# A four-layer graph network on one core: layer 0 adds its rows into a table of x, and layer 1 normalises what it gathers

## The reference

```python
h = relu(layernorm(x)); x = x + L0(h)   # two products and segment sums over dst, relu of each
h = relu(layernorm(x)); x = x + L1(h)   # sum of neighbours, relu(h @ W1.T + b1) @ W2.T + b2, layernorm
h = relu(layernorm(x)); x = x + L2(h)
h = relu(layernorm(x)); x = x + L3(h)

def gnn_layer(x, W, b, src, dst):       # L0 is this twice, with W1 and W2
    h = x @ W.T + b
    agg = segment_sum(h[src], dst)
    return relu(agg)
```

## Time and profile before

| | us |
|---|---|
| time, median of 3 | 2800.5 (2799.15 to 2801.04) |
| span of the profiled execution | 2943.3 |
| p, 0 to 62 | 62 |
| r, 62 to 323 | 261 |
| o, 323 to 384 | 61 |
| a, 384 to 712 | 328 |
| b, 712 to 1175 | 463 |
| c, 1175 to 1774 | 599 |
| d, 1774 to 2363 | 589 |
| f, 2363 to 2943 | 580 |

### The profile page before, as it was taken

The page is one execution under the profiler, slowest core; times in us unless marked ns, Lnnn a source line. Parts: engine busy times, 40 slices in busy tenths (PEclk is TensorE's granted clock), DMA queues, the critical chain, the costliest instruction groups (busy, mean ns, idle before and its releaser), DMA issues. The chain is left out here.

```text
span 2943.3 us, 48010 instructions
## 1 busy us (share of the span) xinstructions
PE 2538.7 (86%) x13886; PEld 2157.9 (73%) x13886; DVE 2010.9 (68%) x5233; ACT 1401.3 (48%) x2905; POOL 1737.8 (59%) x1867
## 2 busy tenths in 40 slices
PE   4555269997878776799999987999999979999998
PEld 3444158886767665799999986888888768888886
DVE  7777656663545444487878886888888846666666
ACT  1555235543656554555555533433333245555554
POOL 1666335554565555577777756877777555555554
PEclk9999999998999898899999998999999989999999
DMA  8777533334333443434334324433333245555553
GB/s 251 203 206 208 159 106 112 111 119 121 104 113 119 129 129 106 126 116 131 109 114 121 112 73 129 129 117 113 115 116 109 80 135 156 151 152 153 151 154 116
DMA packets 146046, 388.08 MB, mean 132 GB/s; under 512 B 34372, under 2 KB 34692, under 8 KB 145315
## 3 DMA queue, kind: packets, MB, share of 16 engines
q0 software_dynamic: 101408, 304.38, 35.0%
q1 hardware_dynamic: 43442, 80.04, 8.9%
q10 hardware_dynamic: 1056, 2.10, 0.2%
HBM read 261.83 MB, written 149.12 MB: 140 GB/s over the span
## 5 line engine op out<-in xcount | busy, mean ns | idle before, releaser
L824 PE MATMUL b_po<-parts,b_Thi 128*128 128x512 f32 x320 | 144.7, 452 | 72.0 <-issue 40.9
L1565 PE MATMUL c_pu<-c_Zhi,parts 128*128 128x256 f32 x640 | 182.9, 286 | 5.3 <-DVE c_Zlo L1490 5.3
L1567 PE MATMUL c_pu<-c_Zhi,parts 128*128 128x256 f32 x640 | 182.4, 285 | 0.0
L1566 PE MATMUL c_pu<-c_Zlo,parts 128*128 128x256 f32 x640 | 181.3, 283 | 0.0
L845 POOL DMA_INDIRECT f_Gsrc<-rows,indexS x80 | 79.2, 990 | 167.3 <-PE f_phsrc L2061 161.3
L1979 ACT ACTIVATE f_Mhi<-f_pm 128x512 fp32r<-128x512 f32 x80 | 47.9, 599 | 266.4 <-DVE f_pm L2012 259.8
L2003 DVE TENSOR_TENSOR f_Hlosrc<-f_phsrc,f_Hhisrc 128x512 fp32r<-128x512 f32 x80 | 55.4, 692 | 168.0 <-ACT f_Hhisrc L1973 137.3
L814 DVE SCALAR_TENSOR_TENSOR b_carry<-b_carry,keylastD,b_pt 128x4 f32<-128x4 f32 x80 | 17.4, 218 | 212.6 <-PE b_pt L1282 127.8
L1727 ACT CAST d_Hhi<-d_ph 128x512 fp32r<-128x512 f32 x80 | 46.8, 585 | 227.3 <-PE d_ph L1841 222.3
L849 POOL DMA_INDIRECT h<-a_rows,indexD x80 | 80.5, 1006 | 124.0 <-ACT a_rows L1148 116.5
L1457 ACT ACTIVATE c_pu<-c_pu,c_b1col 128x256 f32<-128x256 f32 x160 | 61.8, 450 | 164.6 <-PE c_pu L1567 164.6
(11 more groups left out here) (461 smaller groups left out, 9817.4 us busy)
## 6 DMA issues: line engine op xcount, KB each, us to landing
rows<-r_xt SPq DMA_DIRECT2D x40, 520.0 KB
h<-q_zerorow SPq DMA_DIRECT2D x80, 256.0 KB
r_xt<-in_x SPq DMA_DIRECT2D x80, 256.0 KB
selrowsD<-selD SPq DMA_DIRECT2D x1, 2640.0 KB
selrowsS<-selS SPq DMA_DIRECT2D x1, 2640.0 KB
q_keyrowD<-in_dst POOLq DMA_DIRECT2D x1, 2560.0 KB, 17.8
q_keyrowS<-in_src POOLq DMA_DIRECT2D x1, 2560.0 KB
o_wstage<-in_L_W ACTq DMA_DIRECT2D x2, 1024.0 KB
```

What stands on the lines that cost most here:

```text
L824: ins = pe.matmul(out, hi[:, c, :], whi[:, c, :], start=start and c == 0, stop=False, skip_group_check=preset)
L1565: pe.matmul(psum_u[:, o, :], g.Whi[2][:, c, cols], Zhi[:, c, :], start=c == 0, stop=False)
L1566: pe.matmul(psum_u[:, o, :], g.Whi[2][:, c, cols], Zlo[:, c, :], start=False, stop=False)
L1567: ins = pe.matmul(psum_u[:, o, :], g.Wlo[2][:, c, cols], Zhi[:, c, :], start=False, stop=c == C - 1)
```

## The change

- In r the pass over x is gone: its loads, statistics and stores. SP only writes zeros.
- Table `rows1` is replaced by `plain1`, with rows of 512, a row of zeros and 512 spare rows behind.
- In o the index column of the D order names for each row either its node or, where the row isn't the last of its key, a spare row: four small DVE steps more.
- In a, POOL gathers rows of x itself, eight tiles ahead. DVE takes statistics of each gathered tile, POOL makes scales and biases for four tiles at a time, and ACT normalises with them. SP copies x into `plain1` with 80 DRAM-to-DRAM transfers.
- In b, no row of x is gathered and nothing is normalised. POOL adds the relu'd rows to `plain1` with an accumulating indirect DMA (`add_rows`), tile by tile. The selection matrix is made by DVE in one operation (`select`) in place of two on ACT.
- In c, G and X come 512 wide from `plain1`. DVE takes the statistics of both, POOL makes four columns of scales and biases per pair (`scales_in`), and the second bias is put into PSUM by ACT ahead of the product (`preset`) and no longer added by DVE.
- d and f only change the names of their tables.

```diff
-                def statistics_x(T):
-                    dve.wait_ge(q_x[T.slot(RX)], 16 * (T.use(RX) + 1))
-                    ln.statistics(dve, T, xt[:, T.slot(RX), 0:D])
...
+def add_rows(pool, table, at_rows, rows):
+    return pool.indirect_dma_start(table, bass.IndirectOffsetOnAxis(ap=at_rows, axis=0), rows, None,
+                                   compute_op=ALU.add)
...
+                for t in range(NT):
+                    sp.wait_ge(s_rows, t + 1)
+                    sp.dma_start(g.x1[t * P:(t + 1) * P, :], io.x[t * P:(t + 1) * P, :]).then_inc(s_copy, 16)
...
-                if second:
-                    for u in range(RING):
-                        if u % QUAD == 0:
-                            at(i, u, -QUAD, RING, NT, scales)
-                        at(i, u, 4, RING, NT, start_fetch)
-                        at(i, u, 2, RING, NT, residual)
-                        at(i, u, -QUAD, RING, NT, store)
...
+                for u in range(U):
+                    at(i, u, -2, U, NT, store)
+                    if not second and (u + 3) % 4 == 0:
+                        at(i, u, 3, U, NT, scales)
+                    at(i, u, RG, U, NT, start_fetch)
...
-                dve.scalar_tensor_tensor(rows[:, r, 0:D], psum_o[s][:, :], 0.0, xr[x][:, :],
-                                         ALU.max, ALU.add).then_inc(s_rows, 1)
+                dve.tensor_scalar(rows[:, r, :], psum_o[s][:, :], 0.0, None, ALU.max).then_inc(s_rows, 1)
...
+            def scales_in(T):
+                J = item(T, 0)
+                some = slice(J.slot(8), J.slot(8) + 4)
+
+                wait(pool, s_Gn, T.t - 2)
+                wait(pool, s_own, T.t - 2)
+                ln_in.make_scales(pool, J, neg_half, scale_in[:, some])
+                ln_in.make_biases(pool, J, scale_in[:, some], bias_in[:, some])
...
                     at(i, pair, -2, U, NT, lengths_y)
+                    at(i, pair, 6, U, NT, scales_in)
                     for u in (pair, pair + 1):
                         at(i, u, 4, U, NT, keep_x)
...
+            def preset(T):
+
+                wait(act, s_rows, T.t - 3)
+                nc.scalar.copy(psum_o[T.slot(4)][:, :], b2[:, :]).then_inc(s_preset, 1)
...
-                dve.tensor_tensor(o, o, b2[:, :], ALU.add).then_inc(s_biased, 1)
...
+                    for u in (pair, pair + 1):
+                        at(i, u, 6, U, NT, norm_in)
+                        at(i, u, 6, U, NT, finish_in)
```

More of the change, by code:

```diff
@@ L331, in _ @@
                         sp.dma_start(g.sorted[k][row:row + 1, 0:1], sentinel[:, :]).then_inc(q_end, 16)
[L334 to L360, removed]
+                for rows in g.xs:
+                    sp.dma_start(rows[N + 1 - P:N + 1, :], zero_row[:, :]).then_inc(q_end, 16)
+                sp.dma_start(g.x1[N:N + 1, :], zero_row[0:1, 0:D]).then_inc(q_end, 16)
+                for n in range(ADD_RING):
+                    sp.dma_start(g.x1[N + 1 + n * P:N + 1 + (n + 1) * P, :], zero_row[:, 0:D]).then_inc(q_end, 16)
+                for t in range(NT // 2, NT):
+                    sp.wait_ge(q_pos["S"], 2 * (t - NT // 2) + 1)
+                    sp.dma_start(g.h1[t * P:(t + 1) * P, :], zero_row[:, 0:D]).then_inc(q_zero, 16)
                 sp.wait_ge(q_zero, 16 * NT)
-                sp.wait_ge(q_end, 16 * 7)
+                sp.wait_ge(q_end, 16 * (7 + ADD_RING))
             @block.vector
@@ L387, in pick @@
                             .then_inc(q_pos[k], 1)
-                def statistics_x(T):
-                    dve.wait_ge(q_x[T.slot(RX)], 16 * (T.use(RX) + 1))
-                    ln.statistics(dve, T, xt[:, T.slot(RX), 0:D])
[L393 to L398, removed]
-                def body(i):
[L401 to L409, removed]
-                straight(NT // RX, 1, 1, body)
+                def body(i):
+                    for u in range(U):
+                        at(i, u, 1, U, NT, before)
+                        at(i, u, 0, U, NT, pick)
+                straight(GR, 1, 1, body)
             @block.gpsimd
@@ L988, in layer0 @@
             s_preset = e.sem("s_preset")
-        neg_half = e.sb("neghalf", [P, QUAD], F32)
-        G = e.ring("G", U, [P, D if second else EXT], F32)
+        G = e.ring("G", RG, [P, D], F32)
+        if not second:
+            ln = Norm(e, "ln", True, 4)
+            neg_half = e.sb("neghalf", [P, 4], F32)
+            scale_in, bias_in = e.sb("scalein", [P, 8], F32), e.sb("biasin", [P, 8], F32)
         sel = e.ring("sel", 2, [P, P], F32)
@@ new lines, in scales @@
+            def scales(T):
+                some = slice(T.slot(8), T.slot(8) + 4)
+                wait(pool, s_Gn, T.t - 4)
+                ln.make_scales(pool, T, neg_half, scale_in[:, some])
+                ln.make_biases(pool, T, scale_in[:, some], bias_in[:, some])
+            def body(i):
+                for u in range(U):
+                    at(i, u, -2, U, NT, store)
+                    if not second and (u + 3) % 4 == 0:
+                        at(i, u, 3, U, NT, scales)
+                    at(i, u, RG, U, NT, start_fetch)
@@ L1081, in _ @@
-            pool.wait_ge(s_const, 4 if second else 3)
-            straight(NT // RING, 1, 1, body, between=W and (lambda i: W.low_part(pool, i)))
+            pool.wait_ge(s_const, 3)
+            straight(NT // RING, 2, 1, body, between=W and (lambda i: W.low_part(pool, i)))
             for s in range(RING):
@@ L1169, in _ @@
             else:
-                pipeline(act, GR, 1, 1, body, between=lambda i: W.high_part(act, i), first=2 * C + 2)
+                straight(GR, 2, 1, body, between=lambda i: W.high_part(act, i))
         @block.vector
@@ L1495, in norm_y, with norm_in, finish_in @@
             def norm_y(T):
-                o = psum_o[T.slot(4)][:, :]
                 dve.wait_ge(s_prod, T.t + 1)
-                dve.tensor_tensor(o, o, b2[:, :], ALU.add).then_inc(s_biased, 1)
-                dve.wait_ge(s_biased, T.t + 1)
-                ln_y.statistics(dve, T, o)
+                ln_y.statistics(dve, T, psum_o[T.slot(4)][:, :])
+            def norm_in(T):
+                s = T.slot(U)
+                for n, landed, tile in ((0, s_G, G), (1, s_X, X)):
+                    J = item(T, n)
+                    dve.wait_ge(landed[s], 16 * (T.use(U) + 1))
+                    wait(dve, ln_in.s_mean, J.t - 1)
+                    dve.sem_inc(tick, 1)
+                    ln_in.statistics(dve, J, tile[s][:, :])
+            def finish_in(T):
+                for n in range(2):
+                    ln_in.finish(dve, tick, item(T, n))
             def center(T):
```

230 lines of the change are left out of this document (82 added, 148 removed).

## The result

The changed kernel takes 2905.9 us (median of 4, 2904.03 to 2908.98) against 2800.26: the ratio is 1.0382, with a 95% interval of 1.0369 to 1.0395, slower by 105.6 us. The forecast was 2873, slower, with a range of 2750 to 2905. The side and the main mechanism hold; the size is 33 us short, and the time lies 0.9 us beyond the range.

The account below looks back on a forecast made before the run. PE was taken to pace a, c, d and f, something else r and b. Terms of -35 (r), +1 (o), +6 (a), -30 (b), +126 and +5 (c) gave +73 on 2800.5: 2873 us, range 2750 to 2905.

Parts of the forecast that it names:

- The ring in c: In c, POOL's power waits for DVE's variances of tiles POOL gathered last pass: 17.1 us a pair against 13.95, +126.
- the start: In c, statistics and power come ahead of the first sum: +5 us.
- The 142.8 us: Profiled span above the median before the change, assigned to that execution alone: 103 us in b, 40 in r.
- Rival 1: b's late starts also occur in timed executions and the change removes them: 2770 us, faster; chance 0.28.
- The gain is between 0 [...] and 56. I take 35: In r, removing the pass over x leaves POOL's transfers, 205 us against 261: taken as -35.
- the transfers' 205: In r, POOL's two indirect transfers a tile over 80 tiles take 205 us.
- +6: In a, first gather, statistics, POOL's power and ACT delay the start: +6 us, between 3 and 25.
- the 80 copies of SP add [...] to a DMA share of 0.35; hidden: In a, SP's copies add 2 × 256 KB a tile to the DMA load at no cost in time.
- It just fits: In a, DVE's added 1.0 us a tile fits its 1.04 us of waiting for PE, within the 3.86 us tile.
- -30: b, without the 103 us, goes from 360 to 330 us: -30, between -10 and -45.
- rival 3: In b, a slow accumulating transfer sets the pace if over 15 us; at 20 us, 2965 us in total; chance 0.04.
- c's long landing: In c, gathers land 3.48 us after the issue, making the cost +160 instead of +126.

Follow-up runs that it names:

- Experiment 1: Two reorderings of POOL's pass in c of the changed kernel: gathers right behind `scales_in`, 2793.6 us; only `scales_in` moved behind the gathers, 2887.81 us.
- experiment 3: Second bias in c back from ACT to DVE: against the changed kernel, 2911.53 us; against that kernel with gathers right behind `scales_in`, 2839.52 us.
- the second profile: The kernel before, unchanged, profiled once more: span 2799.7 us.
- experiment 8: a's bias put into PSUM by ACT, not added by DVE, against the changed kernel with c's gathers earlier and x copies in r: 2788.21 us.

## Why the prediction was right and wrong

- **The ring in c: the mechanism right, the total right to 1 us partly by luck.** Forecast 17.1 us a pair and +131 with the start; measured +131.5. Link by link, in the pair shown: from the power to the first store 1410.09 - 1404.39 = 5.70 (forecast 5.65), first store to the last gather's issue 1417.52 - 1410.09 = 7.43 (7.43), landing 2.88 (2.53), statistics to the next power 1.40 (1.43): 17.41. Only the landing, taken from one row of another stage, was off. The mean of 16.96 is nearer to 17.1 because it holds the short first and last steps. So the ring costs 39 x (16.96 - 13.97) = 117 us where the text had 126, and the start makes up for it: the first `c_XB` stands 25.1 us behind c's first gather instead of 10.6, +14.5 where the text had +5. Experiment 1 shows that the ring is the cause, and experiment 3 that DVE's load is not. What the text missed is the second ring at 16.65 us. It is hidden in this change, but a repair that opens the first alone gains 18 us.
- **The 142.8 us: right in place and size.** Forecast 103 in b and 40 in r; the second profile has b shorter by 102 us, and the last work of r's DVE earlier by 323.06 - 282.91 = 40.2. Rival 1, which took b's part as real, is out. The Trainium skill, "Perfetto Trace Analysis", section "Tensor Engine Instruction (MATMUL, LD_WEIGHTS)", on ends that are estimated, could not decide this; the second profile did. One sign was wrong: the span was to stand about 40 us above the median in the changed kernel too, and it stands 1 us above. The 40 belonged to the one execution, as the 103 did.
- **r: the step that failed most.** "The gain is between 0 [...] and 56. I take 35" was read off 261 us, though the same text had just assigned 40 us of r to that one execution. Of the 221 us that were left, with the transfers' 205 as the floor, only 16 could go. With o, r gave 15.5. The row with POOL's transfers was right; the number beside it had to be 221.
- **a: +17.5 instead of +6.** The start came as forecast: the first carry was 354.5 - 344 = 10.5 us into a, now 345.2 - 328.5 = 16.7, +6.2. What was put at zero costs 11: the pace, by first and last carry, is (658.7 - 354.5) / 79 = 3.851 before and (660.3 - 345.2) / 79 = 3.989 after. The step "the 80 copies of SP add [...] to a DMA share of 0.35; hidden" failed: with the copies away the pace is (654.7 - 345.2) / 79 = 3.918, 5.6 us less over the stage. Of the other 5.3 us some 3 are a slower steady pace, 3.913 against 3.873, of which more below; the rest stands in the first ten tiles. "It just fits" in DVE held, by experiment 8.
- **b: -25.5 instead of -30**, inside its bounds. Its steady tile went from 4.04 to 3.91 us, and the forecast had 3.9.
- **The accumulate (rival 3): out.** It needed 15 us for an add, and an add takes 4.8; the medians with and without it are 3 us apart. The Trainium skill, "Collectives: The Full Stack", section "The bandwidth ceiling: the fold count and why AG ≠ RS ≠ AR", puts the adding step of a collective at two source reads and about half the rate of a copy. No run here is a collective; for this kernel's indirect transfers the trace agrees in direction: for the same 132 to 133 GB/s the DMA engines are busy 0.74 of b with the add and 0.42 without.
- **Sum and range.** 18.5 us from r and o, 11.5 from a, 4.5 from b and 0.5 from c make 35. Against this, d and f together are 0.8 shorter, and the table's sum of 107.2 stands 1.6 above the 105.6 of the medians, which leaves the 33 us. Each of the three big ones lies in bounds that the text gave itself (r from 0, a up to 25, b from 10), but the range's upper end took only c's long landing, and that not in full: 160 in place of 126 gives 2907 and not 2905. With r at its low end beside it, the range would have held the result with room.

## What to carry to other kernels

When a step that needs what an engine itself has asked for is put into that engine's strict order, add up the way round: issue, landing, the other engine's work, and everything between the wait and the next request. If that is longer than the pace, the order of the requests decides, and a second engine's order can close the same ring again; put the next requests ahead of all that waits. Before a term is read from a stage, set the profiled span beside the median, and where they differ, take the room that is left of that stage and not its length. And where a sum comes out right, compare its terms: here two of c's, 9 us too much and 9.5 us too little, gave a total right to 1 us.

## What the runs showed of the hardware

- Two executions of the same program under the profiler had spans of 2943.3 and 2799.7 us. In the first, DVE started 4.5 us after the recorded end of the sum that it waited for the earlier trace rows; in the second, PE is idle for 1.6 us in all in b's inner 320 us (690 to 1010).
- PE's step in a changed although PE is back to back in both. In the second profile of the kernel before two of a's products start at these times:

```profile
500.39 0.39 PE L824 MATMUL a_po<-parts,a_Thi 128*128 128x512 f32 x1
500.62 0.39 PE L825 MATMUL a_po<-parts,a_Thi 128*128 128x512 f32 x1
```

and in the changed kernel:

```profile
500.08 0.39 PE L795 MATMUL a_po<-parts,a_Tlo 128*128 128x512 f32 x1
500.31 0.40 PE L793 MATMUL a_po<-parts,a_Thi 128*128 128x512 f32 x1
```

Over longer stretches the steps are 0.230 and 0.233 us at a granted clock of 1.00 (501.54 - 500.39 over five steps, and 501.48 - 500.08 over six); for twelve products that makes 0.04 us, and the steady tile went from 3.873 to 3.913. The kernel before had the 0.233 in b and the 0.230 in a. a's program is also unrolled now where it was a loop; which of it makes the step was not tried.
- An accumulating indirect transfer takes POOL 1.58 us to issue for 128 rows of 512, a plain one 1.01; from issue to landing they take 4.8 and 2.8 us (medians of 80).
- The engine that waits for a gather of 128 rows of 512 starts 2.9 us after the end of the gather's issue (1417.52 to 1420.40, in c of the changed kernel).
